# AdaLN/FFN with two adapter layers on one core: slot indices by one load, paced weight chunks, a bias folded to 64 partitions

## The chip, the cores and the metric

One Trainium2 chip, one NeuronCore of it. The metric is the device time of one execution in microseconds (us); lower is better. Engines: TensorE (PE, its weight loads PEld), VectorE (DVE), ScalarE (ACT), GpSimd (POOL) and SyncE (SP), which here does nothing but issue DMAs.

## The reference

The input x is (8 samples, 128 tokens, 512). Two layers follow each other without a nonlinearity, and the result is added to x:

```python
# layer 1: base product plus the adapter that each sample picks from 32 slots
y = x @ W.T + b  +  2.0 * (x @ lora_As[adapter_mapping]) @ lora_Bs[adapter_mapping]
# layer 2: base product plus 8 expert adapters of rank 16, weighted by a top-2 router
base   = y @ W_base.T + b_base
rw,sel = top_k(y @ W_router.T, 2);  w = softmax(rw) scattered over the 8 experts
lora   = sum_e w[e] * (y @ A[e].T) @ B[e].T * 2.0
out    = x + base + lora
```

## The kernel before

**What is tiled.** Nothing lies between the layers, so the kernel multiplies the weights together first. C is the second layer's right side: 280 columns of W_base.T, 8 router columns, 128 expert columns, 232 more of W_base.T, 648 in all (WC). `wt` holds W and C in four chunks of 128 rows, k = 0 to 3, each row also with the first layer's bias b repeated (CB = 1164 columns, 582 KB a chunk). Every operand is split into a rounded "high" part (fp32r) and a "low" remainder, and each product is three matmuls: high by high, high by low, low by high.

**The order on TensorE** is written out by hand, in stages:
1. 28 idle matmuls, then M = W.T C, per chunk k 24 matmuls (line 567). Chunk 0 comes in four pieces, of which SP and ACT issue two each. The last chunk goes block by block (i = 0 to 3), so that ACT can copy block i out of PSUM as high part (`bm`, `am`, line 330) and VectorE form its low part (line 408).
2. G = B-adapters by C, 24 matmuls (line 628, "the G product"). It waits for the adapters' high and low parts and for `m_lo_done` 2, the low parts of block 0 of M, since it writes in PSUM where that block stood.
3. The bias product (line 639): ones by `bsum_hl`, two column ranges, high and low: 4 matmuls. `bsum` is the sum over k of C row by b of that row (line 413, on VectorE, 4 steps), a matmul with ones adds up its 128 partitions. The second layer's bias b_base is put into `bsum`'s row 0 by a DMA ahead of the first step, on a tile that GpSimd has set to zero.
4. Per sample: `routed` (line 661, 12 matmuls of 384 columns) with router, expert and adapter columns; `plain` (line 673); the slot product (lines 696 and 701), which adds G's rows of the sample and the bias rows, both from the stack `g_st`; the transposes and the expert product (line 721). VectorE adds x (line 520), SP writes out.

**SP's queue** is one list in program order: pieces of w0, then w1, b_base, w2, w3, x0 (the transposed x of samples 0 and 1, 512 KB), then for each sample a load of its slot index into a register (line 233) and the DMA of its adapter (line 234, 64 KB), then x1, b_t, x2, x3 (lines 236 to 239). Later: 12 DMAs that build `g_st`, two that write bias rows to it (line 258), x by rows, and the outputs. Each DMA has a semaphore that the reader waits for.

**ACT's queue** around the change: high parts of chunks 1 to 3, of x0, of the adapters, of `bsum`, then of the blocks of M, of x1, of b_t, of G, of the bias product. **VectorE's**: low parts of the chunks with a bias step between, `bs_lo`, then the low parts of M, with `bsum`'s after block 1. **GpSimd**: waits for `bs_lo_done` and forms the adapters' low part (line 308), puts adapters beside M (line 304) and forms the low parts of x (line 297); `routed(0)` waits for the first two of these.

Of the kernel before, what the change touches and what calls it, by code (L numbers as in the profile page):

```python
# [32 lines left out]
P = 128  # L33
# [11 lines left out]
AHEAD = 4  # L45
CH = D + WC
# [10 lines left out]
GK = CROW + 2  # L57
# [11 lines left out]
def build(nc, x, xn_in, w, tbl, idx, bbase, bt, out):  # L69
    with ExitStack() as ctx:  # L70
# [29 lines left out]
        bsum_hl = sb("bsum_hl", [P, 2, WC], F32R)  # L100
# [10 lines left out]
        hw = sb("hw", [P, PAIRS, 2, P])  # L111
        hw_hi = sb("hw_hi", [P, NB, P], F32R)
# [49 lines left out]
        bsum_zero = sem("bsum_zero")  # L162
# [22 lines left out]
        m_lo_done = sem("m_lo_done")  # L185
        bsum_done = sem("bsum_done")
        bsum_hi_done = sem("bsum_hi_done")
# [3 lines left out]
        g_lo_done = sem("g_lo_done")  # L191
        c_done = sem("c_done")
# [27 lines left out]
        def _(sp):  # L220
# [15 lines left out]
            sp.dma_start(xt[:, 1], x[:, 1]).then_inc(x_in[1], 16)  # L236
            sp.dma_start(btt[:], bt).then_inc(bt_in, 16)
            for p in range(2, PAIRS):
                sp.dma_start(xt[:, p], x[:, p]).then_inc(x_in[p], 16)

            for p in range(PAIRS):
                rows = slice(2 * R * p, 2 * R * (p + 1))
                if p == 0:
                    sp.wait_ge(g_hi_done, 2)
                sp.dma_start(g_st[0:LROW, p, :].bitcast(F32),
                             g_hl[rows, 0, :].bitcast(F32)).then_inc(gst_in[p], 16)
                sp.dma_start(g_st[HROW:CROW, p, :].bitcast(F32),
                             g_hl[rows, 0, :].bitcast(F32)).then_inc(gst_in[p], 16)
                if p == 0:
                    sp.wait_ge(g_lo_done, 2)  # L250
                sp.dma_start(g_st[LROW:HROW, p, :].bitcast(F32),
                             g_hl[rows, 1, :].bitcast(F32)).then_inc(gst_in[p], 16)
                if p == 0:

                    sp.wait_ge(c_hi_done, 2)
                    sp.wait_ge(c_lo_done, 2)
                    for i in range(2):
                        sp.dma_start(g_st[CROW + i:CROW + i + 1, :, :].bitcast(F32),
                                     bsum_hl[0:1, i:i + 1, :].bitcast(F32).to_broadcast([1, PAIRS, WC])
                                     ).then_inc(cst_in, 16)  # L260
# [16 lines left out]
        def _(pool):  # L277
            nc.gpsimd.memset(bsum[:], 0.0).then_inc(bsum_zero, 1)
# [27 lines left out]
            pool.wait_ge(bs_lo_done, 1)  # L306
# [21 lines left out]
        def _(act):  # L328
# [11 lines left out]
            hi(wt_hi[:, 0, D + QB:CH], wt[:, 0, D + QB:CH]).then_inc(wc_hi_done, 1)  # L340

# [14 lines left out]
            x_high(0)  # L356
# [17 lines left out]
            for s, c in enumerate(COLS):  # L374
                hi(bsum_hl[0:1, 0, c], ps[0:1, C_BANK + s, 0:c.stop - c.start]).then_inc(c_hi_done, 1)
# [22 lines left out]
        def _(dve):  # L398
# [11 lines left out]
            def bias_sum(k):  # L410
                if k > 0:
                    dve.wait_ge(bsum_done, k)
# [15 lines left out]
            for k in range(1, KB):  # L428
# [10 lines left out]
                if k == 1:  # L439
                    dve.wait_ge(bbase_in, 16)  # L440
                bias_sum(k - 1)
            bias_sum(KB - 1)
            dve.wait_ge(ab_hi_done, 1)
            lo(bs_lo[:].rearrange("p k b r -> p b k r"), ab[:, :, 1],
               bs_hi[:].rearrange("p k b r -> p b k r")).then_inc(bs_lo_done, 1)

            for i in range(KB):
                if i == 2:
                    dve.wait_ge(bsum_hi_done, 1)
                    lo(bsum_hl[:, 1], bsum[:], bsum_hl[:, 0]).then_inc(bsum_lo_done, 1)  # L450
# [3 lines left out]
                lo(am[:, i, 1, R:R + WA], ps[:, 2 * i + 1, 0:WA], am[:, i, 0, R:R + WA]).then_inc(m_lo_done, 1)  # L454
            for s, c in enumerate(COLS):
                dve.wait_ge(g_hi_done, s + 1)
                lo(g_hl[:, 1, c], ps[:, G_BANK + s, 0:c.stop - c.start], g_hl[:, 0, c]).then_inc(g_lo_done, 1)
            for s, c in enumerate(COLS):
                dve.wait_ge(c_hi_done, s + 1)
                lo(bsum_hl[0:1, 1, c], ps[0:1, C_BANK + s, 0:c.stop - c.start],  # L460
                   bsum_hl[0:1, 0, c]).then_inc(c_lo_done, 1)
# [96 lines left out]
        def _(pe):  # L558
# [258 lines left out]
```

## Time and profile before

| what | value |
|---|---|
| times of three runs | 66.97, 67.73, 67.77 us, median 67.73 |
| the profiled execution | 67.57 us |
| its span, first to last instruction | 65.8 us |
| outside the span | 1.8 us |
| busy: PE, VectorE, ACT, GpSimd | 61.9, 35.9, 21.5, 17.0 us |
| granted TensorE clock over the span | 1.00, also in the 40 slices |

The span is the part that the rows explain; the time is the span and 1.8 us around it. A matmul's row shows its own duration, but matmuls overlap, so what one costs the stream is the distance from start to start. Positions below are microseconds from the start of the span.

### The profile page before, as it was taken

To read this page: it belongs to the slowest core of one execution; us is meant where nothing else is said; L and a number is where in the kernel's file an instruction comes from. 1 tells how busy PE (TensorE), PEld (TensorE's weight loads), DVE (VectorE), ACT (ScalarE), POOL (GpSimd) and SP (SyncE) were. 2 spreads that over 40 slices of the span, in tenths; PEclk is the share of its full clock that TensorE was granted. 3 is DMA by queue.
4 is the path that set the end of the run, shared out by engine and by line. 5 is a ranking of instruction groups with operands and counts; after the bars stand their busy time and mean duration, and the time that the engine had idled before them with its cause. 6 is when DMAs were issued, how large, how long until landed. Compare 5 with 4: busy or idle time off the path is not lost.

```text
span 65.8 us, 1181 instructions
## 1 busy us (share of the span) xinstructions
PE 61.9 (94%) x424; PEld 60.8 (92%) x424; DVE 35.9 (55%) x103; ACT 21.5 (33%) x46; POOL 17.0 (26%) x30
## 2 busy tenths in 40 slices
PE   5999979999999999999999999999999999999930
PEld 5979879999999999998999999999999999999920
DVE  0056289998599667015935495002668363857320
ACT  0660358905989399127104100010201040020000
POOL 6810000000699982695390000010100000000000
PEclk9999999999999999999999999999999999999999
DMA  0899998219999004245559999700044000013532
GB/s 0 247 376 259 393 411 262 71 54 175 217 356 369 25 0 101 60 104 129 123 136 339 275 283 401 267 15 0 0 159 159 10 0 0 0 66 123 215 146 87
DMA packets 5865, 10.55 MB, mean 160 GB/s; under 512 B 731, under 2 KB 2523, under 8 KB 5860
## 3 DMA queue, kind: packets, MB, share of 16 engines
q1 hardware_dynamic: 5570, 10.15, 48.0%
q10 hardware_dynamic: 290, 0.33, 1.5%
q8 instruction: 3, 0.05, 0.3%
q14 instruction: 2, 0.02, 0.1%
HBM read 7.37 MB, written 2.10 MB: 144 GB/s over the span
## 4 chain that ended last, share of the span: by engine, by line
PE 83%; DMA 9%; SPq 1%; ACT 1%; DVE 1%; issue 1%
PE ps L661 26%; PE ps L673 19%; PE ps L567 17%; DMA wt<-w_chunks 9%; PE ps L721 9%; PE ps L628 5%; PE ps L696 2%; PE ps L701 2%; PE ps L684 1%; PE ps L707 1%; SPq L223 1%; ACT wt_hi L330 1%; PE ps L639 1%; DVE xn L520 1%
## 5 line engine op out<-in xcount | busy, mean ns | idle before, releaser
L661 PE MATMUL ps<-am,x_hi 128*128 128x384 f32 x64 | 16.6, 340 | 0.0
L673 PE MATMUL ps<-bm,x_hi 128*128 128x280 f32 x64 | 13.0, 297 | 0.0
L661 PEld LDWEIGHTS ps<-am,x_hi 128*128 128x128 f32 x64 | 11.4, 188 | 0.0
L661 PE MATMUL ps<-am,x_lo 128*128 128x384 f32 x32 | 10.8, 338 | 0.0
L297 POOL TENSOR_TENSOR x_lo<-xt,x_hi 128x512 fp32r<-128x512 f32 x8 | 10.8, 1367 | 0.0
L673 PEld LDWEIGHTS ps<-bm,x_hi 128*128 128x128 f32 x64 | 10.2, 188 | 0.0
L673 PE MATMUL ps<-bm,x_lo 128*128 128x280 f32 x32 | 9.3, 291 | 0.0
L567 PE MATMUL ps<-wt_hi 128*128 128x280 f32 (+1 forms) x32 | 7.4, 327 | 0.5 <-ACT wt_hi L330 0.3
L520 DVE TENSOR_TENSOR xn<-ps,xn 128x280 f32<-128x280 f32 (+1 forms) x16 | 6.1, 418 | 2.4 <-PE ps L721 2.3
L567 PE MATMUL ps<-wt_lo,wt_hi 128*128 128x280 f32 (+1 forms) x32 | 7.0, 316 | 0.0
L567 PE MATMUL ps<-wt_hi,wt_lo 128*128 128x280 f32 (+1 forms) x32 | 6.5, 310 | 0.0
L408 DVE TENSOR_TENSOR wt_lo<-wt,wt_hi 128x512 fp32r<-128x512 f32 (+3 forms) x9 | 5.9, 689 | 0.8 <-ACT wt_hi L330 0.8
L304 POOL CAST am<-as_hl 128x128 fp32r<-128x128 f32 x8 | 2.3, 293 | 15.4 <-PE ps L661 15.4
L567 PEld LDWEIGHTS ps<-wt_hi 128*128 128x128 f32 x32 | 5.4, 196 | 1.0 <-DVE wt_hi L431 0.6
L673 PEld LDWEIGHTS ps<-bm,x_lo 128*128 128x128 f32 x32 | 6.0, 188 | 0.0
L330 ACT ACTIVATE hw_hi<-ps 128x256 fp32r<-128x256 f32 x4 | 1.5, 384 | 13.7 <-PE ps L707 13.7
L661 PEld LDWEIGHTS ps<-am,x_lo 128*128 128x128 f32 x32 | 6.0, 188 | 0.0
L330 ACT ACTIVATE wt_hi<-wt 128x648 fp32r<-128x648 f32 (+3 forms) x8 | 4.3, 573 | 4.1 <-DMA wt<-w_chunks 4.1
L567 PEld LDWEIGHTS ps<-wt_lo,wt_hi 128*128 128x128 f32 x32 | 5.4, 195 | 0.0
L408 DVE TENSOR_TENSOR hw_lo<-ps,hw_hi 128x256 fp32r<-128x256 f32 x4 | 1.7, 425 | 6.7 <-ACT hw_hi L330 6.7
L567 PEld LDWEIGHTS ps<-wt_hi,wt_lo 128*128 128x128 f32 x32 | 5.1, 188 | 0.0
L308 POOL TENSOR_TENSOR as_hl<-ab,as_hl 128x512 fp32r<-128x512 f32 x1 | 1.3, 1302 | 13.3 <-DVE bs_lo L408 13.3
(70 smaller groups left out, 98.5 us busy)
## 6 DMA issues: line engine op xcount, KB each, us to landing
xt<-x_t SPq DMA_DIRECT2D x4, 512.0 KB, 6.5
xn<-x_n SPq DMA_DIRECT2D x4, 512.0 KB, 6.0
out_n<-xn SPq DMA_DIRECT2D x7, 256.0 KB, 2.0
wt<-w_chunks SPq DMA_DIRECT2D x3, 582.0 KB, 6.6
g_st<-g_hl SPq DMA_DIRECT2D x12, 81.0 KB, 2.1
ab<-adapters SPq DMA_DIRECT2D x8, 64.0 KB, 2.7
wt<-w_chunks SPq DMA_DIRECT2D x2, 128.0 KB, 2.9
btt<-b_t SPq DMA_DIRECT2D x1, 256.0 KB, 5.0
```

What stands on the lines that cost most here:

```text
L297: nc.gpsimd.tensor_tensor(x_lo[:, p, k, :], xt[:, p, k, :], x_hi[:, p, k, :].bitcast(F32), ALU.subtract).then_inc(x_lo_done, 1)
L304: nc.gpsimd.tensor_copy(am[:, :, :, at:at + R], as_hl[:, b].bitcast(F32)).then_inc(as_put, 1)
L330: return nc.scalar.activation(dst, src, ACT.Copy)
L408: return nc.vector.tensor_tensor(dst, src, high.bitcast(F32), ALU.subtract)
L520: nc.vector.tensor_tensor(xn[:, b, c], src, xn[:, b, c], ALU.add).then_inc(out_ready, 1)
L567: return mm(ps[:, 2 * i + s, 0:cols.stop - cols.start], a[:, k, i * P:(i + 1) * P], c[:, k, D + cols.start:D + cols.stop], start=first, st ...
L628: last = mm(ps[:, G_BANK + s, 0:c.stop - c.start], a[:, k].rearrange("p b r -> p (b r)"), v[:, k, D + c.start:D + c.stop], start=(k == 0 a ...
L661: last = mm(a_bank(b)[:, 0:R + WA], v[:, p, i, tok], am[:, i, level, at:at + R + WA], start=(i == 0 and n == 0), stop=False, skip_group_ch ...
L673: mm(b_bank(b)[:, 0:QB], v[:, p, i, tok], bm[:, i, level, :], start=(i == 0 and n == 0), stop=False, skip_group_check=True)
L696: last = mm(a_bank(2 * p + t)[:, at:at + WA], h_t[0:GK, p, t, :], g_st[0:GK, p, QB:WC], start=False, stop=False, skip_group_check=True)
L701: mm(b_bank(b)[:, 0:QB], h_t[0:GK, b // 2, b % 2, :], g_st[0:GK, b // 2, 0:QB], start=False, stop=False, skip_group_check=True)
L721: last = mm(dst, v[:, b, :], m[:, c], start=False, stop=(n == 2), skip_group_check=True)
```

## The change

It does five things.
1. SP reads all eight slot indices by one load and then issues the eight adapter DMAs one behind the other.
2. SP issues w1, waits for the first piece of w0 (`w0_in[0]`), issues w2, waits for the indices and reads them, issues w3, then the adapters, and only then x0, x1, b_t, x2, x3 and b_base. ACT takes the adapters ahead of x0 to match.
3. The first bias step (k = 0) is an ACT activation with a scale per partition, so `bsum` need not be zero at the start; GpSimd's memset of it goes. VectorE keeps steps 1 to 3.
4. VectorE folds `bsum` to 64 partitions: it copies the upper half down (64x648), adds it, and the high part goes to partitions 0 to 63 and the low part to 64 to 127 of one tile `bsum_st`. The bias product is then 2 matmuls, not 4. High and low are made ahead of those of M, and GpSimd now starts after `bsum_lo_done`.
5. b_base goes to a row of its own. Its high part (ACT) and low part (VectorE) are formed after those of M and sent as two more rows of `g_st`, so the slot product has 100 rows, not 98, and waits for four such DMAs.

```diff
@@ SP @@
-            for k in range(1, KB):
-                sp.dma_start(wt[:, k, :], w[:, k, :]).then_inc(w_in[k], 16)
-                if k == 1:
-                    sp.wait_ge(bsum_zero, 1)
-                    sp.dma_start(bsum[0:1, :], bbase).then_inc(bbase_in, 16)
-            sp.dma_start(xt[:, 0], x[:, 0]).then_inc(x_in[0], 16)
-
+            sp.dma_start(wt[:, 1, :], w[:, 1, :]).then_inc(w_in[1], 16)
+            sp.wait_ge(w0_in[0], 16)
+            sp.dma_start(wt[:, 2, :], w[:, 2, :]).then_inc(w_in[2], 16)
             sp.wait_ge(idx_in, 16)
-            for b in range(NB):
-                slot = sp.value_load(idx_sb[0:1, b:b + 1], min_val=0, max_val=SLOTS - 1)
+            _, slots = nc.values_load_multi_w_load_instructions(
+                idx_sb[0:1, :], engines=[mybir.EngineType.SP], min_val=0, max_val=SLOTS - 1)
+            sp.dma_start(wt[:, 3, :], w[:, 3, :]).then_inc(w_in[3], 16)
+            for b, slot in enumerate(slots):
                 sp.dma_start(ab[:, b].rearrange("p c k r -> p (c k r)"),
                              tbl[bass.ds(slot, 1)].rearrange("s p n -> (s p) n")).then_inc(ab_in, 16)
+            sp.dma_start(xt[:, 0], x[:, 0]).then_inc(x_in[0], 16)
             sp.dma_start(xt[:, 1], x[:, 1]).then_inc(x_in[1], 16)
             sp.dma_start(btt[:], bt).then_inc(bt_in, 16)
             for p in range(2, PAIRS):
                 sp.dma_start(xt[:, p], x[:, p]).then_inc(x_in[p], 16)
+            sp.dma_start(bb, bbase).then_inc(bbase_in, 16)
+            sp.wait_ge(bb_hi_done, 1)
+            spread(CROW, bb_hl[:, 0:1, :])
+            sp.wait_ge(bb_lo_done, 1)
+            spread(CROW + 1, bb_hl[:, 1:2, :])
@@ ACT @@
+            act.wait_ge(w0_in[2], 16)
+            nc.scalar.activation(bsum[:], wt[:, 0, D:CH], ACT.Copy,
+                                 scale=wt[:, 0, CH:CH + 1]).then_inc(bsum_first, 1)
...
-            x_high(0)
             act.wait_ge(ab_in, 16 * NB)
             hi(bs_hi[:].rearrange("p k b r -> p b k r"), ab[:, :, 1]).then_inc(ab_hi_done, 1)
             hi(as_hl[:, :, :, 0, :], ab[:, :, 0]).then_inc(ab_hi_done, 1)
-            act.wait_ge(bsum_done, KB)
-            hi(bsum_hl[:, 0], bsum[:]).then_inc(bsum_hi_done, 1)
+            x_high(0)
+            act.wait_ge(halves_done, 1)
+            hi(bsum_st[0:HP], bsum[0:HP]).then_inc(bsum_hi_done, 1)
...
+            act.wait_ge(bbase_in, 16)
+            hi(bb_hl[:, 0], bb).then_inc(bb_hi_done, 1)
             x_high(1)
@@ VectorE @@
-                bias_sum(k - 1)
+                if k > 1:
+                    bias_sum(k - 1)
             bias_sum(KB - 1)
+            dve.wait_ge(bsum_done, KB - 1)
+            nc.vector.tensor_copy(upper, bsum[HP:P]).then_inc(upper_done, 1)
+            dve.wait_ge(upper_done, 1)
+            nc.vector.tensor_tensor(bsum[0:HP], bsum[0:HP], upper, ALU.add).then_inc(halves_done, 1)
             dve.wait_ge(ab_hi_done, 1)
             lo(bs_lo[:].rearrange("p k b r -> p b k r"), ab[:, :, 1],
                bs_hi[:].rearrange("p k b r -> p b k r")).then_inc(bs_lo_done, 1)
+            dve.wait_ge(bsum_hi_done, 1)
+            lo(bsum_st[HP:P], bsum[0:HP], bsum_st[0:HP]).then_inc(bsum_lo_done, 1)
 
             for i in range(KB):
-                if i == 2:
-                    dve.wait_ge(bsum_hi_done, 1)
-                    lo(bsum_hl[:, 1], bsum[:], bsum_hl[:, 0]).then_inc(bsum_lo_done, 1)
...
+            dve.wait_ge(bb_hi_done, 1)
+            lo(bb_hl[:, 1], bb, bb_hl[:, 0]).then_inc(bb_lo_done, 1)
@@ GpSimd @@
-            nc.gpsimd.memset(bsum[:], 0.0).then_inc(bsum_zero, 1)
...
-            pool.wait_ge(bs_lo_done, 1)
+            pool.wait_ge(bsum_lo_done, 1)
@@ TensorE @@
-                for i in range(2):
-                    last = mm(ps[:, C_BANK + s, 0:c.stop - c.start], ones_r[:], bsum_hl[:, i, c],
-                              start=(i == 0), stop=(i == 1))
+                last = mm(ps[:, C_BANK + s, 0:c.stop - c.start], ones_r[:], bsum_st[:, c], start=True, stop=True)
...
-                    pe.wait_ge(cst_in, 32)
+                    pe.wait_ge(cst_in, 64)
```

SP's queue at the head of the program, before: `w_chunks` are w1 and, behind b_base, w2 and w3; ISA rows are register operations on a slot index.

```order
L225 DMA wt<-w_chunks 128x1164
L228 DMA bsum<-b_base 1x648 [waits bsum_zero]
L225 DMA wt<-w_chunks 128x1164 x2
L229 DMA xt<-x_t 128x1024
L233 TENSOR_LOAD idx_sb [waits idx_in]
L233 ISA x2
L234 ISA
L234 DMA ab<-adapters 128x128
L233 TENSOR_LOAD idx_sb
```

And the same place in the changed kernel:

```order
L233 DMA wt<-w_chunks 128x1164
L235 DMA wt<-w_chunks 128x1164 [waits w0_in0]
L237 TENSOR_LOAD idx_sb [waits idx_in]
L237 ISA x16
L239 DMA wt<-w_chunks 128x1164
L241 ISA
L241 DMA ab<-adapters 128x128
```

b_base and x0 have left this place. The eight loads have become one with sixteen register operations, and these stand ahead of w3's issue and of all adapters; x0's issue follows the eighth adapter.

ACT's queue from chunk 3 to the first block of M, before (`bs_hi` and `as_hl` are the adapters, `bm` and `am` block 0 of M):

```order
L330 ACTIVATE wt_hi<-wt 128x648 [waits w_in3]
L330 ACTIVATE wt_hi<-wt 128x512
L330 ACTIVATE x_hi<-xt 128x512 [waits x_in0]
L330 ACTIVATE x_hi<-xt 128x512
L330 ACTIVATE bs_hi<-ab 128x8x4x16 [waits ab_in]
L330 ACTIVATE as_hl<-ab 128x32x16
L330 ACTIVATE bsum_hl<-bsum 128x648 [waits bsum_done]
L330 ACTIVATE bm<-ps 128x280 [waits m_done]
```

And in the changed kernel:

```order
L345 ACTIVATE wt_hi<-wt 128x648 [waits w_in3]
L345 ACTIVATE wt_hi<-wt 128x512
L345 ACTIVATE bs_hi<-ab 128x8x4x16 [waits ab_in]
L345 ACTIVATE as_hl<-ab 128x32x16
L345 ACTIVATE x_hi<-xt 128x512 [waits x_in0]
L345 ACTIVATE x_hi<-xt 128x512
L345 ACTIVATE bsum_st<-bsum 64x648 [waits halves_done]
L345 ACTIVATE bm<-ps 128x280 [waits m_done]
```

The wait for x0 has moved behind the one for the adapters; it is now the last DMA wait in the queue ahead of the bias and of block 0 of M.

## Rows read from the trace of the kernel before

**Rows 1.** The chain in order of time: start us, length us, what.

```profile
1.66 6.05 DMA wt<-w_chunks
...
8.62 10.92 PE ps L567 x72
19.54 3.56 PE ps L628 x24
23.10 0.60 PE ps L639 x4
```

**Rows 2.** Timeline of PE and PEld at chunk 1 and G: start, length, what, idle before.

```profile
6.95 1.34 PE L567 MATMUL ps<-wt_hi,wt_lo 128*128 128x280 f32 x8
8.62 0.75 PE L567 MATMUL ps<-wt_hi 128*128 128x280 f32 x4 [0.33 <-ACT wt_hi L330]
...
19.21 0.19 PEld L628 LDWEIGHTS ps<-wt_hi,bs_hi 128*128 128x128 f32 x1
```

**Rows 3.** DMA queues, window 0 to 5.5 us: packets, MB, share of 16 engines.

```profile
q1 hardware_dynamic: 430, 0.86, 53.0%
```

**Rows 4.** Timeline of SP's queue: x0, the adapters, x1.

```profile
3.39 1.13 SPq L229 DMA_DIRECT2D xt<-x_t  x1
5.56 8.44 SPq L234 DMA_DIRECT2D ab<-adapters  x8
14.04 0.43 SPq L236 DMA_DIRECT2D xt<-x_t  x1
```

**Rows 5.** Source lines 233 and 234: ns min/median/max, first and last start.

```profile
L233 SPq TENSOR_LOAD <-idx_sb x8: 262/269/487, 4.6 to 12.6; - x8
L233 SPq FUSED_REGOPS  x8: 152/152/192, 5.1 to 12.9; - x8
...
L234 SPq FUSED_REGOPS  x8: 42/42/48, 5.4 to 13.1; - x8
...
L234 SPq DMA_DIRECT2D ab<-adapters x8: 337/338/714, 5.6 to 13.3; - x8
```

**Rows 6.** Issue to landing, line 225: w1, w2, w3.

```profile
DMA to landing us min/median/max: 6.0/6.6/7.7
```

**Rows 7.** Issue to landing, line 236: x1.

```profile
DMA to landing us min/median/max: 4.9/4.9/4.9
```

**Rows 8.** Issue to landing, line 262, window 32.9 to 33.5: the first of x by rows.

```profile
DMA to landing us min/median/max: 3.8/3.8/3.8
```

**Rows 9.** Issue to landing, line 239: x2 and x3, issued at 15.0 and 15.5.

```profile
DMA to landing us min/median/max: 6.2/6.5/6.9
```

**Rows 10.** Timeline of ACT: start, length, what, idle before it.

```profile
9.19 1.27 ACT L330 ACTIVATE wt_hi<-wt 128x648 fp32r<-128x648 f32 x2 [0.71 <-DMA wt<-w_chunks]
10.64 1.27 ACT L330 ACTIVATE wt_hi<-wt 128x648 fp32r<-128x648 f32 x2 [0.18 <-DMA wt<-w_chunks]
11.96 1.16 ACT L330 ACTIVATE x_hi<-xt 128x512 fp32r<-128x512 f32 x2
...
16.56 0.73 ACT L330 ACTIVATE bsum_hl<-bsum 128x648 fp32r<-128x648 f32 x1
...
23.14 0.77 ACT L330 ACTIVATE g_hl<-ps 128x280 fp32r<-128x280 f32 x2 [1.22 <-PE ps L628]
```

**Rows 11.** Timeline of VectorE: the last chunk's bias steps, block 0 of M.

```profile
14.16 1.81 DVE L413 SCALAR_TENSOR_TENSOR bsum<-wt,bsum 128x648 f32<-128x648 f32 x2
...
17.61 0.45 DVE L408 TENSOR_TENSOR bm<-ps,bm 128x280 fp32r<-128x280 f32 x1 [0.75 <-ACT bm L330]
17.98 0.54 DVE L408 TENSOR_TENSOR am<-ps,am 128x368 fp32r<-128x368 f32 x1
```

**Rows 12.** Groups by form: busy us, mean ns of one, idle before.

```profile
L408 DVE TENSOR_TENSOR wt_lo<-wt,wt_hi 128x648 fp32r<-128x648 f32 x3 | 2.5, 827 | 0.3 <-ACT wt_hi L330 0.3
L431 DVE CAST wt_hi<-wt 128x512 fp32r<-128x512 f32 x1 | 0.4, 427 | 1.5 <-DMA wt<-w_chunks 1.5
```

**Rows 13.** Timeline of GpSimd: the adapters' low part.

```profile
16.95 1.30 POOL L308 TENSOR_TENSOR as_hl<-ab,as_hl 128x512 fp32r<-128x512 f32 x1 [13.34 <-DVE bs_lo L408]
```

More of the change, by code:

```diff
@@ L45 @@
 AHEAD = 4
+HP = P // 2
 CH = D + WC
@@ L56 @@
 LROW, HROW, CROW = 2 * R, 4 * R, 6 * R
-GK = CROW + 2
+GK = CROW + 4
 AW = R + WA + R
@@ L99, in build @@
         bsum = sb("bsum", [P, WC])
-        bsum_hl = sb("bsum_hl", [P, 2, WC], F32R)
+        bsum_st = sb("bsum_st", [P, WC], F32R)
+        cb_hl = sb("cb_hl", [HP + 1, 2, WC], F32R)
+        c_hl, bb_hl = cb_hl[0:1], cb_hl[HP:HP + 1]
         h_stack = sb("h_stack", [P, PAIRS, 2 * HSTEP])
@@ L111, in build @@
         hw = sb("hw", [P, PAIRS, 2, P])
+        hw_flat = hw[:].rearrange("p a t c -> p (a t c)")
+        upper, bb = hw_flat[0:HP, 0:WC], hw_flat[HP:HP + 1, 0:WC]
         hw_hi = sb("hw_hi", [P, NB, P], F32R)
@@ L160, in build @@
         bbase_in = sem("bbase_in")
-        bsum_zero = sem("bsum_zero")
         const = sem("const")
@@ L185, in build @@
         m_lo_done = sem("m_lo_done")
+        bsum_first = sem("bsum_first")
         bsum_done = sem("bsum_done")
+        upper_done = sem("upper_done")
+        halves_done = sem("halves_done")
         bsum_hi_done = sem("bsum_hi_done")
@@ L191, in build @@
         g_lo_done = sem("g_lo_done")
+        bb_hi_done = sem("bb_hi_done")
+        bb_lo_done = sem("bb_lo_done")
         c_done = sem("c_done")
@@ L239, in _, with spread @@
                 sp.dma_start(xt[:, p], x[:, p]).then_inc(x_in[p], 16)
+            sp.dma_start(bb, bbase).then_inc(bbase_in, 16)
+            def spread(row, src):
+                sp.dma_start(g_st[row:row + 1, :, :].bitcast(F32),
+                             src.bitcast(F32).to_broadcast([1, PAIRS, WC])).then_inc(cst_in, 16)
+            sp.wait_ge(bb_hi_done, 1)
+            spread(CROW, bb_hl[:, 0:1, :])
+            sp.wait_ge(bb_lo_done, 1)
+            spread(CROW + 1, bb_hl[:, 1:2, :])
             for p in range(PAIRS):
@@ L257, in _ @@
                     for i in range(2):
-                        sp.dma_start(g_st[CROW + i:CROW + i + 1, :, :].bitcast(F32),
-                                     bsum_hl[0:1, i:i + 1, :].bitcast(F32).to_broadcast([1, PAIRS, WC])
-                                     ).then_inc(cst_in, 16)
+                        spread(CROW + 2 + i, c_hl[:, i:i + 1, :])
             for p in range(PAIRS):
@@ L374, in _ @@
             for s, c in enumerate(COLS):
-                hi(bsum_hl[0:1, 0, c], ps[0:1, C_BANK + s, 0:c.stop - c.start]).then_inc(c_hi_done, 1)
+                hi(c_hl[0:1, 0, c], ps[0:1, C_BANK + s, 0:c.stop - c.start]).then_inc(c_hi_done, 1)
             x_high(2)
@@ L410, in bias_sum @@
             def bias_sum(k):
-                if k > 0:
-                    dve.wait_ge(bsum_done, k)
+                if k == 1:
+                    dve.wait_ge(bsum_first, 1)
+                else:
+                    dve.wait_ge(bsum_done, k - 1)
                 nc.vector.scalar_tensor_tensor(out=bsum[:], in0=wt[:, k, D:CH], scalar=wt[:, k, CH:CH + 1],
@@ L438, in _ @@
                 lo(wt_lo[:, k, 0:D], wt[:, k, 0:D], wt_hi[:, k, 0:D]).then_inc(w_lo_done, 1)
-                if k == 1:
-                    dve.wait_ge(bbase_in, 16)
-                bias_sum(k - 1)
+                if k > 1:
+                    bias_sum(k - 1)
             bias_sum(KB - 1)
+            dve.wait_ge(bsum_done, KB - 1)
+            nc.vector.tensor_copy(upper, bsum[HP:P]).then_inc(upper_done, 1)
+            dve.wait_ge(upper_done, 1)
+            nc.vector.tensor_tensor(bsum[0:HP], bsum[0:HP], upper, ALU.add).then_inc(halves_done, 1)
             dve.wait_ge(ab_hi_done, 1)
@@ L459, in _ @@
                 dve.wait_ge(c_hi_done, s + 1)
-                lo(bsum_hl[0:1, 1, c], ps[0:1, C_BANK + s, 0:c.stop - c.start],
-                   bsum_hl[0:1, 0, c]).then_inc(c_lo_done, 1)
+                lo(c_hl[0:1, 1, c], ps[0:1, C_BANK + s, 0:c.stop - c.start],
+                   c_hl[0:1, 0, c]).then_inc(c_lo_done, 1)
             dve.wait_ge(bt_hi_done, 1)
```

## The prediction

> **What bounds the kernel now.** Read the chain of waits first, in order of time [rows 1]. It opens with a DMA, chunk w1, from its issue at 1.66 to its landing 6.05 later, at 7.71. From 8.62 on the chain is matmuls with hardly a break: M to 19.54, the G product to 23.10, the bias product to 23.70, then the samples. So the time is where TensorE starts chunk 1, plus the length of its stream, plus any wait inside it. Everything else counts only if it becomes such a wait.
>
> Then read TensorE's timeline at chunk 1 [rows 2]. The 8 last matmuls of chunk 0 start at 6.95. A full third of a chunk (8 matmuls) takes 10.92 / 9 = 1.21 us of stream [rows 1], so they leave the stream free at about 8.15, and chunk 1 starts at 8.62. The gap is 0.47 us, and w1's landing with ACT's high part behind it ends it. That is all that an earlier w1 can give.
>
> **The change, part by part.** The sum is made against the profiled 67.57 us.
>
> *Bias product, 4 matmuls to 2.* The four took 0.60 us of stream [rows 1]; one of each width goes, so half: **-0.30 us**, on the chain. This one is sure.
>
> *Pacing, for w1.* To start chunk 1 at 8.15, w1 must be in by about 7.2, since from its landing to the first matmul of chunk 1 it was 0.91 us (7.71 to 8.62). Between **0 and -0.47 us**. For a gain: 0.86 MB had passed SP's queue by 5.5 us [rows 3], which is its two pieces of w0 (0.26 MB) and w1 (0.60 MB), yet w1 landed at 7.71. Some of its transfers were held up while w2, w3 and x0 lay behind it; with w2 issued 1 us later and the others much later, the hold-up may go. Against it: w2 is issued before w1 is through in either kernel. I can't choose by these rows; what each end makes of the sum shows below, where a later wait takes a part of it back.
>
> On this point the Trainium skill, DMA: Bandwidth & Descriptors, section Queues, rings and completion order, says that each DMA engine consumes a ring's descriptors in ring order. By that rule what is queued behind w1 can't slow it and pacing gives 0; the trace agrees in the bytes of [rows 3], not in the landing 2.2 us after them. By the rule the sum would be 67.3; if the landing row is right and the hold-up goes, 67.1.
>
> *Index load and the queue on SP.* This is where I look for the cost. Before, the adapters' issues were 7.7 / 7 = 1.10 us apart [rows 5], of which the load is 0.27, the register operation on it 0.15, the one on the address 0.04 and the issue 0.34; the remaining 0.30 is an assert, a move and the gaps. Now: w2's issue ends at about 4.0; the first load started at 4.6, when x0's issue had ended, so the indices are in by then, and I take 4.6. The load takes 0.49 as the first did: 5.1. Then eight pairs of register operations. Upper bound 0.15 + 0.12 a value, 2.2 us in all; lower bound, if the 0.15 was mostly a wait for the load, 0.04 + 0.12, 1.3 us. I take 1.8: w3 is issued at 6.9 instead of about 3, and takes 0.47. Eight adapters at 0.04 + 0.34 + 0.15 = 0.53 are 4.2: x0 is issued at **11.5**, not at 3.39 [rows 4]. The ends are 11.1 and 12.0.
>
> *When x0 lands, and who waits.* The nearest row is x1 before: 512 KB too, issued at 14.04 right behind the adapters' trickle, landed 4.9 us later [rows 4, 7]. The next is the first x by rows, into an idle queue: 3.8 [rows 8]. As a lower bound: ACT took w2 and w3 at 9.19 and 10.64 [rows 10], 1.45 a chunk when queued back to back, so 512 KB move in 1.3; an adapter of 64 KB was in by about 2.2 (the last issued at 13.3, waited for until 15.5), which makes 3.3. I take 3.9, between the two rows nearer the quicker one, because the queue is never quite empty now: x0 lands at **15.4** (14.4 to 16.9).
>
> Behind x0 in ACT's queue stand its own high part, the bias, and block 0 of M, and behind these, in VectorE's, bias low, `bm` low, `am` low; the G product waits for the last of them. From the landing: x0's two operations 1.08 (1.16 less the overlap) [rows 10], the bias high part 0.73, its low part 0.83 [rows 12], `bm` to `am` 0.37 and `am` 0.54 [rows 11], and about 0.08 of hand-over: **3.63 us**. So G can start at 15.4 + 3.63 = 19.0. TensorE's first weight load of G stood at 19.21 [rows 2], right behind the last of M, and comes at 18.74 if w1 gives its 0.47. Thus G is held to about 19.0 with an early w1, and not held with a late one (19.21). The gain at G is 0.2 or 0: with the bias product, **-0.5 or -0.3**; I take -0.4.
>
> *Bias chain.* VectorE loses one step of 0.9 (half of 1.81 [rows 11]); ACT takes it at 0.75 while it waits for w1 anyway. Added are a copy of 64x648 (0.50: 427 ns for 512 columns [rows 12], scaled), an addition and a low part at 0.83 each, against a low part of 648 columns that stood between blocks 1 and 2 of M. The chain after w3: ACT 0.76, VectorE 1.43 of low parts, bias steps 1.8, copy and addition 1.3: 5.3. With w3 landing at 10.6 as before, and VectorE busy with chunk 2 until then, the halves are done between 16.2 and 16.9; x0's high part is through at 16.5. The two arrive together, so neither hides more than some 0.4 us of the other's lateness. GpSimd starts when `bsum_lo` is done, at about 18.1, not 16.95 [rows 13]. Its 5 us until the first two low parts of x were ready by 21.9 and needed at 23.5; now 23.1 against a need at about 22.9 to 23.1 (G at 19.0 to 19.2, its 3.56 and the bias product's 0.30 [rows 1]). Taken as 0, bound +0.3.
>
> *b_base.* It is last in SP's line, behind x3, which landed at 15.5 + 6.9 = 22.4 [rows 9]; x1 to x3 now follow x0 from 12 on, so x3 and b_base come at about 21.5. ACT reaches the wait at about 20.3 and stands; then b_base high 0.7, x1 1.1, b_t 0.6, so G's high part starts at 23.9 instead of 23.14 [rows 10], where 1.22 us were idle. The bias rows reach `g_st` that much later; they had over 1 us in hand before the first slot product (landing about 28.7, product at 30.15). I take 0, bound +0.8. SP's two more DMAs of 0.65 fall where it waits for G. Two more rows in the slot product add no columns: 0.
>
> Sum: 67.57 - 0.30 - 0.1 = **67.2 us**. The profiled execution lies 0.16 below the median of the runs, so a median may come out at 67.3 as well. What a measurement of this kernel can tell from no change is about 2%, here 1.35 us.
>
> **Rivals.**
>
> *A, everything in time.* w1 lands by 7.2 and x0 by 15.1, as it would at 11.5 + 3.3 = 14.8. Then -0.47 and -0.30: 66.8. For it the bytes of [rows 3]; against it x1's 4.9 us. The Trainium skill, DMA: Bandwidth & Descriptors, section Anatomy of one DMA, gives 2.0 us plus bytes over 436 GB/s (a fit for GpSimd's path); an estimate by that page is 3.2 us for 512 KB, x0 in at 14.7. The trace does not agree for x1 (4.9) or the first x by rows (3.8).
>
> *B, no earlier w1, x0 in time.* The change does not do what its pacing says: 67.3, all from the bias product. It lies so close to the forecast that only the trace tells them apart: chunk 1 still starts near 8.6.
>
> *C, slower: x0 gates G.* x0's landing repeats x1's 4.9 us: in at 16.4, or 16.9 with the late issue. G starts at 20.0 to 20.5, 0.8 to 1.3 after 19.21; less 0.30: 68.1 to 68.6, say 68.2. It costs more than the change brings from a landing at about 15.9 on. For it: the nearest row of all, with the same trickle ahead. Against it: x0 itself moved at full rate when it followed the chunks. A w3 that takes its 6.6 us [rows 6] from 6.9 on would land at 13.5 and do the same through the bias chain, its limit being about 11.6; then 69 or more.
>
> *D, b_base holds the first slot product.* b_base in after 22.4: at 23.2, 0.8 us of wait: 68.0.
>
> **How the numbers follow.** The forecast, x0 near 15.4 so that G starts at 19.0 to 19.2, 0.25; B 0.25 (its time, 67.3, falls in the forecast's own 67.0 to 67.4, so that 67.2 is the likeliest time with 0.5); A 0.17; C 0.25, of which 0.07 by w3 and dearer than 2%; D 0.08. Eight in ten lie between 66.4 and 68.8: A with a little more at the low end, C with the late issue at the high end. Faster by over 2% (below 66.4) would need more than A: 0.06. Slower by over 2% (above 69.1): 0.10. Within: 0.84.
>
> **What would show it.** Right: the bias product's row x2 and 0.30; SP's x0 issue between 11.1 and 12.0 and its landing in 3.3 to 4.9; one block of register operations of 1.3 to 2.2 between load and w3. If G's first matmul starts later than chunk 3's last by more than 0.17, x0 or the halves gate it, and ACT's idle time ahead of `x_hi` or `bsum_st` tells which. Wrong: a TensorE wait anywhere else (first slot product: D; `routed(0)`: GpSimd), or an x0 issued before 10, which would mean that I have misread the register operations. The prediction fails if w3 lands after 11.6, or if the stream's start moves by more than the 0.47 us that the gap holds.

## The result and the profile after

| | before | after |
|---|---|---|
| first comparison, 4 runs each | median 67.64 us (66.97 to 67.77) | 68.87 us (68.12 to 70.84) |
| ratio, 95% interval | | 1.018 (1.010 to 1.026) |
| the same two kernels again (a0) | 67.36 us, 13 runs | 69.12 us, 5 runs; 1.026 (1.017 to 1.035) |
| the profiled execution: time, span, outside it | 67.57, 65.8, 1.8 us | 70.84, 68.7, 2.1 us |

The changed kernel is slower, by about 2%. The forecast of 67.2 us was wrong. The mechanism that came true is rival C, with two costs on top that no case held. In the profiled execution the granted clock fell for 3.4 us. That cost 1.6 us and explains 70.84 (last section); the other three had a clock of 1.0 over the span and took 68.12, 68.66 and 69.08. The medians here and below hold all executions; the ratios compare fast ones with fast ones, so without those in which the clock fell.

The chain of the changed kernel in order of time (start, length, what), to be held against [rows 1]:

```profile
11.76 5.57 DMA xt<-x_t
17.35 1.15 ACT x_hi L345 x2
21.07 5.34 PE ps L653 x24
26.71 5.26 PE ps L684 x30
```

In [rows 1] only matmuls stand from 8.62 to 23.70. Here the chain leaves TensorE, goes through x0's DMA from its issue at 11.76 to its landing at 17.33, and comes back at the G product, 21.07. SP's queue shows how x0 came to be issued there [rows 4 for before]:

```profile
3.42 0.33 SPq L235 DMA_DIRECT2D wt<-w_chunks  x1
7.23 0.33 SPq L239 DMA_DIRECT2D wt<-w_chunks  x1
7.75 3.96 SPq L241 DMA_DIRECT2D ab<-adapters  x8
11.76 0.43 SPq L243 DMA_DIRECT2D xt<-x_t  x1
```

Source line 237, the one load with its register operations (ns, first and last start in us), against [rows 5]:

```profile
L237 SPq FUSED_REGOPS  x8: 147/147/192, 5.1 to 7.0; - x8
L237 SPq SEQ_ASSERT  x8: 18/18/33, 5.4 to 7.2; - x8
L237 SPq TENSOR_LOAD <-idx_sb x1: 729/729/729, 4.4 to 4.4; - x1
```

Source line 243, x0, against [rows 7]:

```profile
DMA to landing us min/median/max: 5.6/5.6/5.6
```

Then ScalarE's timeline, where x0 is waited for, against [rows 10]:

```profile
15.56 0.62 ACT L345 ACTIVATE as_hl<-ab 128x512 fp32r<-128x512 f32 x1
17.35 1.15 ACT L345 ACTIVATE x_hi<-xt 128x512 fp32r<-128x512 f32 x2 [1.17 <-DMA xt<-x_t]
18.41 0.73 ACT L345 ACTIVATE bsum_st<-bsum 64x648 fp32r<-64x648 f32 x1
19.04 0.38 ACT L345 ACTIVATE bm<-ps 128x280 fp32r<-128x280 f32 x1
```

VectorE's, against [rows 11]:

```profile
16.45 0.68 DVE L427 TENSOR_TENSOR bs_lo<-ab,bs_hi 128x512 fp32r<-128x512 f32 x1
19.17 0.83 DVE L427 TENSOR_TENSOR bsum_st<-bsum,bsum_st 64x648 fp32r<-64x648 f32 x1 [2.04 <-ACT bsum_st L345]
20.03 0.45 DVE L427 TENSOR_TENSOR bm<-ps,bm 128x280 fp32r<-128x280 f32 x1
20.39 0.53 DVE L427 TENSOR_TENSOR am<-ps,am 128x368 fp32r<-128x368 f32 x1
```

And TensorE's at the end of M, at G and at the bias product, against [rows 2]:

```profile
18.80 0.33 PE L592 MATMUL ps<-wt_hi,wt_lo 128*128 128x368 f32 x1
21.07 0.37 PE L653 MATMUL ps<-wt_hi,bs_hi 128*128 128x280 f32 x1 [1.94 <-DVE am L427]
...
26.25 0.46 PE L663 MATMUL ps<-bsum_st,ones_r 128*128 128x280 f32 x2
26.55 0.52 PE L684 MATMUL ps<-am,x_hi 128*128 128x384 f32 x2
```

These rows form one staircase. ScalarE stands 1.17 us for x0 while block 0 of M lies ready in PSUM behind it from about 16.4 on (chunk 3 starts at 15.40, and a quarter of it takes 0.9). VectorE stands 2.04 us for ScalarE, and TensorE 1.94 us for VectorE. The bias product is x2 and 0.30 us from start to start, as forecast.

The whole difference in the span, 2.91 us, from positions in the two traces (before, after): chunk 1 starts at 8.62, 8.20: -0.42. M keeps its length. From M's last matmul to G: 0.17, 2.27: +2.10. G: 3.56, 5.18: +1.62 (the clock). Bias product to `routed(0)`: 0.59, 0.30: -0.29. The rest, 42.26 and 42.16: -0.10. Outside the span it is 0.36 more.

### The profile page after: what moved, and what is told of

The parts are those of the page before. It is cut to its first block, busy times and chain, and to the rows that moved or that the text cites. A ratio compares the mean times of both kernels' runs of the same rounds, so it can differ in the third digit from the quotient of the medians.

```text
span 68.7 us, 1175 instructions
## 1 busy us (share of the span) xinstructions
PE 63.2 (92%) x422; PEld 61.9 (90%) x422; DVE 37.6 (55%) x105; ACT 22.8 (33%) x48; POOL 16.5 (24%) x29
## 4 chain that ended last, share of the span: by engine, by line
PE 65%; DMA 12%; SPq 8%; DVE 3%; issue 3%; ACT 3%; ACTq 1%
PE ps L684 25%; PE ps L696 18%; PE ps L744 8%; DMA xt<-x_t 8%; PE ps L653 8%; SPq L241 5%; DMA idx_sb<-slots 4%; SPq L237 3%; PE ps L719 2%; ACT x_hi L345 2%; PE ps L724 2%; PE ps L730 1%; PE ps L707 1%; ACTq L348 1%; DVE bsum_st L427 1%
```

## The experiments

All times are compared within one comparison. "Outside" is the time less the span: 1.73 to 1.83 us in every run of the kernel before.

### Which half of the change: a0, b1, e4, e3

a0 is the changed kernel again, b1 the kernel before; a0's 1.026 stands in the table above.

> The changed kernel unchanged, for its spread and for a second profile. Theory T1: x0, now issued at 11.8 us behind the index load, w3 and eight adapters, lands at about 17.3, and ACT's x0 high part, the bias, and block 0 of M wait behind it, so that the G product starts at landing + 3.7 us. T1 expects that relation again (G's first matmul 3.6 to 3.8 us after x0's landing), whatever the landing is; 1.0 to 1.5% slower than before. Theory T2: the longer bias chain on VectorE (two more steps, and low part ahead of those of M) gates G. T2 expects ACT to have x0's high part ready before the halves are done, and G at halves + 4 us. Second question: the granted clock fell after the 1.9 us wait in the first profile. If the wait alone does it, it falls again; if not in every execution, this profile may show 1.00 and a time near 68.6 us.

b1 had chunk 1 at 8.58, G at 19.36, a span of 65.8 and 67.55 us: the trace of before repeats.

> The kernel before, for a second profile. Its spans in the last comparison fell between 65.0 and 66.0 us, and the share of the time outside the span was 1.73 to 1.82 us in all 13 runs. Theory: the spread comes from the start, where the granted clock rises at another moment and w1 lands at another, so chunk 1 should start between 8.1 and 8.7 us here too, and everything after it take the same time as in the first profile (57.2 us from chunk 1 to the end), within 0.1 us. Rival: the spread comes from waits later in the stream.

e4 is the queue half on the kernel before (load, order of SP, ScalarE's x0 behind the adapters; bias as before):

> Before's bias (4 matmuls, no folding, b_base in row 0 of bsum, 4 steps on VectorE) with the changed DMA order, single index load and ACT order. Theory T1 (the queue costs, the bias part is neutral): x0 issued at about 12.1 (one DMA more ahead), landing at about 17.3, G at landing + 1.1 (x0 high) + 0.7 (bias high) + 1.3 (block 0 high and low) = 20.4, 1.2 us late; time 68.6 to 69.0 us, and the granted clock may fall after the wait. Theory T4: the part of the time outside the span, 2.13 us in every run with the changed bias against 1.77, belongs to the bias part; then it is 1.77 here. If it belongs to the queue part it is 2.13 here (against which e3 speaks already).

**68.35 us, ratio 1.012 (1.006 to 1.017)**, outside 1.73 to 1.81. Its TensorE timeline:

```profile
18.56 0.33 PE L568 MATMUL ps<-wt_hi,wt_lo 128*128 128x368 f32 x1
20.56 0.37 PE L629 MATMUL ps<-wt_hi,bs_hi 128*128 128x280 f32 x1 [1.67 <-DVE am L409]
```

x0 landed at 17.37. So the queue half alone makes the wait.

e3 is the bias half alone, with SP's old queue:

> Before's DMA order and index loads (all chunks and x0 first, one load per slot, x0's high part ahead of the adapters' on ACT) with the changed bias: first step on ACT, folding, two matmuls, b_base as rows, its DMA at the end of the line. T1: the bias part alone is worth its 0.30 us less what the longer chain takes: adapters landed 15.5, ACT free for the bias at 16.6, bias low at 18.1, G at 19.2 to 19.4; time 67.2 to 67.7 us against before's 67.6. T2: G starts after 20, and this kernel carries most of the loss: 68.4 us or more.

67.34 us, 1.002 (0.996 to 1.007). From chunk 1 to the end of the span it took 57.01 us, before 57.17, but outside it 2.09 to 2.21 us.

### Where x0 stands: e1, e5, e2

```diff
@@ e1: SP @@
             sp.dma_start(wt[:, 3, :], w[:, 3, :]).then_inc(w_in[3], 16)
+            sp.dma_start(xt[:, 0], x[:, 0]).then_inc(x_in[0], 16)
             for b, slot in enumerate(slots):
...
-            sp.dma_start(xt[:, 0], x[:, 0]).then_inc(x_in[0], 16)
@@ e5: the same, and on ACT x_high(0) ahead of the adapters @@
@@ e2: SP as changed; on ACT x_high(0) behind the blocks of M @@
```

> The changed kernel with x0's DMA issued right after w3's, ahead of the eight adapters; nothing else moves. T1: x0 is issued at about 7.6 us and lands by 12.5, out of the way; the adapters go 0.47 us later and land by about 15 us, so the bias high part starts when the halves are done (about 16.5), G starts by 19.4 to 19.6, and the time is 66.8 to 67.4 us, 1 to 2 us under the changed kernel. T2: G stays late, at 20.5 or more, and the time above 68 us.

e1: 68.72 us, 1.021 (1.008 to 1.034): I had expected 66.8 to 67.4. x0 landed at 13.06, but ScalarE's queue still had x0 behind the adapters, which landed at 15.39, so both were worked off after 15.39:

```profile
20.19 0.37 PE L653 MATMUL ps<-wt_hi,bs_hi 128*128 128x280 f32 x1 [0.59 <-DVE am L427]
```

The wait at G fell from 1.94 to 0.59 us and did not go: x0 landed 4.3 us earlier, and G gained 1.35. An earlier landing brings only a part where the reader's queue keeps its order.

> The changed kernel with x0 issued ahead of the adapters and with ACT's x0 high part ahead of the adapters' too. In e1 x0 landed at 13.1 but its high part still stood behind the adapters (landed 15.4), so G had to wait for adapters + 1.1 + 1.1 + bias. T1: now only 1.1 (adapters' high parts) stands there, the halves are done at about 17.0, G starts 0.1 to 0.5 us behind the last of M; time 67.3 to 67.8 us, about 1 us under the changed kernel. T2 (the bias chain itself is too long): G still 0.6 us or more behind, 68.2 or more.

e5: with both queues turned, x0 landed at 12.72, and G followed M's last matmul by 0.28 us, not 2.27. 68.02 us, 1.011 (1.004 to 1.017). The ratio stands for about 0.7 us, of which 0.36 is outside the span (2.09 to 2.21) again. The rest, about 0.3 us, I can't assign: from chunk 1 to the end of the span the profiled execution, the fastest of the four, took 56.92 us against 57.17 in before.

> The changed kernel with ACT's high part of x0 moved behind the high parts of M's four blocks; x0 lands as late as in the changed kernel. T1: what cost the time is the position in ACT's queue, not the landing itself, so G starts at about 19.3 (halves done 16.5, bias high and low 1.6, block 0's low parts 1.0, hand-over), and the time is 66.9 to 67.6 us; ACT's x0 part ends at about 21 and GpSimd's low parts of x0 at about 23, just ahead of the first sample's product. T2: no better than the changed kernel. A third theory, T3: the late x0 would then hold routed(0) itself, so that the wait only moves from G to there and the time stays at 68.5.

e2: x0 landed late again, at 17.00, but G was on time (19.21, 0.17 behind M). TensorE's list of waits, 17 to 35 us:

```profile
PE ps L684 <- POOL x_lo L312: 1.0, 1, 1.0
```

The wait has moved to `routed(0)`, which needs the low part of x0. 68.37 us, 1.015 (1.006 to 1.025). e5 and e2 together show that G's wait was x0's high part in ScalarE's queue. The new wait is again one of place in that queue: x0 was in at 17.00, and ScalarE, busy with the four blocks of M, took it up at 20.07. A place between, behind block 0 of M alone, was not tried, so it stays open what a late x0 costs at its best place.

### The parts of the bias half: f1, f2, f3, s1

f1 has the fold alone (b_base in `bsum`'s row 0, four bias steps on VectorE), f2 b_base's rows alone (bias product x4), f3 is f2 with the first step on ScalarE and without GpSimd's memset. s1 adds to before four semaphores and four tiny GpSimd memsets that raise them, and nothing else.

> Before's DMA queue, all four bias steps on VectorE and b_base in bsum's row 0 as before; only the folding to 64 partitions and the bias product of 2 matmuls are new. The changed bias showed 2.09 to 2.21 us outside the span where before shows 1.73 to 1.83, and four more semaphores alone did not (s1: 1.73 to 1.83). Theory T5a: the folding (copy to other partitions, half-height operations) brings it: 2.1 outside. T5b: the rows of b_base or ACT's first step bring it: 1.77 here. On the stream: -0.30 us from the bias product; with one bias step more on VectorE than the changed kernel, the halves are done at 17.2 and G is held 0.3 to 0.6 us; sum about zero, 67.2 to 67.9 us.

f1: 67.37, 1.001 (0.997 to 1.004), outside 1.73 to 1.82. The fold gives its 0.30 and takes it back: its low part is ahead of M's in VectorE's queue, and TensorE waits 0.53 us at G.

> Before's DMA queue and bias product (4 matmuls, no folding, four steps on VectorE from a zeroed bsum), with b_base as two more rows of the slot product, its DMA last in the line. T5b: if these rows bring the 0.36 us outside the span, 2.1 outside and 67.8 to 67.9 us; if not, 1.77 and 67.5. The stream itself should not change, unless ACT's wait for b_base (landing about 21) reaches the first slot product, which I expect it not to.

f2: 68.02, 1.011 (1.002 to 1.021), outside **1.98 to 2.08**.

> f2 with the first bias step on ACT (activation with a scale per partition), no memset of bsum. Theory T5c: this instruction brings the 0.36 us outside the span (2.1 here, 1.77 in f2). If f2 already shows 2.1, then no more here. Time otherwise as f2, VectorE 0.9 us less busy before the G product, which nothing waits for.

f3: 68.12, 1.014 (1.005 to 1.022), outside **2.09 to 2.21**.

> The kernel before with four more semaphores, each raised once by a one-column memset at the end of GpSimd's queue, where it is idle. The changed kernel has four more than before. Theory T4a: the 0.36 us more outside the span are a cost per semaphore (about 0.09 us each), so this kernel shows 2.1 us outside and takes 0.3 to 0.4 us more than before. Rival T4b: they come from something else of the bias part (another kind of instruction, tile sizes); then 1.77 outside, and no difference in time.

s1: 67.24, 0.996 (0.992 to 0.999), outside 1.73 to 1.83. Not the number of semaphores.

### Pacing alone: p1

```diff
                 if k == 1:
...
+                    sp.wait_ge(w0_in[0], 16)
```

> The kernel before with one edit: SP waits for the first piece of w0 before it issues w2 (so w2, w3 and x0 are issued 1 to 1.5 us later). Theory P1 (pacing lets w1 in earlier): w1 lands by 7.1 to 7.4, as in the six paced profiles (7.06 to 7.38), instead of 7.66 to 7.71, chunk 1 starts 0.1 to 0.45 us earlier depending on when the granted clock rises, and the time is 0.2 to 0.3 us under before. Rival P2 (w1's landing varies by itself: two kernels without pacing showed 7.16 and 7.32): no difference of the medians, within 0.1 us.

67.33, 0.999 (0.995 to 1.003). w1 landed at 7.46. In thirteen profiles without pacing it landed anywhere from 7.07 to 8.13, in the seven paced ones between 7.06 and 7.46. Seven of the thirteen lie above 7.46, none of the seven, so w1 does come somewhat earlier when paced. But the time can't be told from no change; the interval leaves room for 0.3 us. One reason is in the other profiles. In six of the thirteen (e3, f2, g2, s1, q1, q2) chunk 1 starts 1.18 to 1.20 us after the last third of chunk 0, so TensorE did not wait for w1 at all, and there was no gap to close.

### What lies outside the span: q1, q2, q3, e6

q1 writes two bias rows more to `g_st` by DMA, in rows that nobody reads. q2 and q3 add to before one dummy activation of 128x512 ahead of w1's high part, with and without a scale per partition; SP waits for it before it issues b_t, whose tile it writes. All three only add work.

> The kernel before with two more bias DMAs on SP, high and low row of bsum copied once more into two rows of g_st that nobody reads, and a wait for them at the end of SP's queue. Dummy work is added and nothing else changes. If the part outside the span grows with the number of DMAs (or semaphores waited for by SP), it is 1.95 to 2.1 us here against 1.73 to 1.83 before; if the b_base rows brought their 0.25 us otherwise, it stays at 1.73 to 1.83. Span unchanged within 0.3 us, ratio 1.003 to 1.006 or 1.000.

q1: 67.13, 0.997 (0.994 to 1.000), outside 1.74 to 1.84: not the DMAs.

```diff
@@ q2: ACT @@
+            act.wait_ge(w0_in[2], 16)
+            nc.scalar.activation(btt[:], wt[:, 0, D:2 * D], ACT.Copy,
+                                 scale=wt[:, 0, CH:CH + 1]).then_inc(scaled, 1)
@@ q3: the same without the scale @@
```

> The kernel before with one more activation on ScalarE: 128x512 of w0 times a scale per partition (the first layer's bias column), written to the b_t tile before b_t's own data are loaded. Dummy work is added and nothing else changes. If an activation with a scale per partition makes the part outside the span longer (it was 0.1 more in the run of rows and ACT step than in rows alone), it is 1.85 us or more here; if that was something else, it stays at 1.73 to 1.83. The activation itself should take about 0.6 us in ScalarE's wait for w1, so the span stays within 0.3 us, ratio 0.998 to 1.006.

q2: 67.62, 1.005 (1.001 to 1.009), outside **1.99 to 2.08**.

> As the run of the scaled activation, with a plain copy of the same 128x512 in its place (no scale per partition). Dummy work is added and nothing else changes. Theory N (the part outside the span goes by the number of ScalarE's activations in the program: 46 gave 1.73 to 1.83 us in seven kernels, 47 gave 1.98 to 2.08, 48 gave 2.09 to 2.21, whatever the activation did): 47 activations, 1.98 to 2.08 us outside. Rival S (the scale per partition brings it): 1.73 to 1.83.

q3: 67.47, 1.002 (0.998 to 1.006), outside **2.02 to 2.08**: the scale is not the cause either. By then the number of activations fitted every kernel, so e6 takes two away from e3 by joining the high parts of x2 and of x3:

```diff
-                for k in range(0, KB, 2):
-                    hi(x_hi[:, p, k:k + 2, :], xt[:, p, k:k + 2, :]).then_inc(x_hi_done, 1)
+                step = KB if p > 1 else 2
+                for k in range(0, KB, step):
+                    hi(x_hi[:, p, k:k + step, :], xt[:, p, k:k + step, :]).then_inc(x_hi_done, step // 2)
```

> The whole bias part of the change with the kernel's old queue (as in e3, 48 activations on ScalarE), but the high parts of x2 and of x3 are one activation of 1024 columns each, not two of 512, so that ScalarE has 46 again. Theory N: outside the span falls from 2.09 to 2.21 to 1.73 to 1.83 us, the span stays that of e3 (chunk 1 to the end about 57.0), median about 67.0, ratio 0.993 to 0.998. Rival (b_base's rows and the first bias step bring it by what they do): it stays at 2.09 to 2.21, ratio 1.000 to 1.003.

e6: 68.05, 1.011 (1.005 to 1.017), outside still 2.09 to 2.17 with 46 activations. So the number of activations does not fit. Two other counts still fit every kernel. One is ScalarE's waits for DMAs: 11 in the kernels with 1.72 to 1.84, 12 in f2, q2 and q3 (1.98 to 2.08), 13 in e3, f3, e6 and the changed kernel with e1, e2 and e5 (2.09 to 2.22). The other is all of ScalarE's instructions in the trace, semaphore waits that stand as instructions of their own included: 53, 54 and 55 in the same groups. e6 did not lower it, since the trace has two such waits ahead of the joined activations (at 23.92 and 24.01) where the two activations went. No run parts the two counts or takes a wait away by itself, so both stay correlations.

### The fold alone, its parts made later: g1, g2

g1 is f1 with the folded bias's high and low parts behind block 1 of M, and GpSimd waits for `bs_lo` again; g2 is g1 with e6's joined activations.

```diff
@@ g1 against f1: ACT @@
-            act.wait_ge(halves_done, 1)
-            hi(bsum_st[0:HP], bsum[0:HP]).then_inc(bsum_hi_done, 1)
             for i in range(KB):
+                if i == 2:
+                    act.wait_ge(halves_done, 1)
+                    hi(bsum_st[0:HP], bsum[0:HP]).then_inc(bsum_hi_done, 1)
```

> The kernel before with the fold alone (b_base in bsum row 0, all bias steps on VectorE, the bias product 2 matmuls), its high and low part made behind block 1 of M and GpSimd released by bs_lo, as before. Theory T (only the PE stream and the waits in it count, the 0.48 us wait of the first fold run was the folded bias standing ahead of M's low parts): the G product starts within 0.2 us of the last matmul of M, bias product 0.30 us, span 0.30 shorter than before at an equal start of chunk 1 (chunk 1 to the end about 56.9, not 57.17), outside the span 1.72 to 1.83, median 67.0 to 67.2, ratio 0.993 to 0.998. Rival R (the bias part arrives later and is waited for between G and the bias product or at the first slot product): G on time but bias product or slot product late by 0.3 or more, ratio 1.00 or above.

> g1 (the fold alone, made behind block 1 of M) with the high parts of x2 and of x3 as one activation each, so ScalarE has 44 activations instead of 46. Theory N with a term per activation: outside the span below 1.73 us, perhaps 1.5 to 1.7, median 66.8 to 67.0, ratio 0.990 to 0.996. Theory N with a step between 46 and 47 only: 1.73 to 1.83, same as g1, ratio 0.996 to 0.999. This is the candidate for a version that beats both kernels.

g1: 67.18 us against 67.26, 0.997 (0.994 to 1.000). g2: 67.17 against 67.43, 0.997 (0.993 to 1.000). In both the G product follows M's last matmul by 0.17 us, and outside is as before, 1.73 to 1.84. g2's chain from chunk 1 on:

```profile
19.79 3.56 PE ps L642 x24
23.34 0.30 PE ps L652 x2
```

Both lie 2 to 3% under the changed kernel, compared through the kernel before. Against the kernel before each interval just reaches 1.000, and s1 and q1, which only add work to it, came out at 0.996 and 0.997 too. So the times show no gain. The traces do: from chunk 1 to the end of the span g1 took 56.99 us and g2 56.69, against 57.17 and 57.19 in the two profiles of before and 57.10 in s1 and q1, but that is one execution each. Two activations fewer changed nothing outside the span; ScalarE's instructions are 53 in g2 as in g1.

## Why the prediction was wrong

**What came as written.** The bias product: 0.30 off, from x4 to x2. SP's queue: the load from 4.38, the block of register operations 2.1 us long (1.3 to 2.2 given, 1.8 taken: the upper bound was right, each of the eight takes 0.15 as a chained one did), w3 issued at 7.23 (6.9), x0 at 11.76 (11.5; 11.1 to 12.0). That the load ended at 5.11, as written, is luck: it took 0.73 us, not 0.49, and began 0.22 earlier than I took. From x0's landing to G 3.74 us (3.63). w3 landed at 11.17, ahead of the 11.6 that was its limit, and the halves were done before x0's high part was. b_base held nothing (D did not occur): G to the first slot product is otherwise unchanged. In the profiled execution chunk 1 started at 8.20, close to the 8.15 of rival A.

**The step that failed: "I take 3.9 ... x0 lands at 15.4."** It is the term for x0's landing; from it the sum had G at 19.0 to 19.2, with no wait. x0 landed 5.6 us after its issue, at 17.33. In e4, a0 and e2, with the same order on SP, it took 5.5, 5.3 and 5.4. I had the nearest row in hand, x1 with 4.9 us behind the same trickle [rows 7], and moved away from it toward a DMA into an idle queue [rows 8] with the reason that the queue is "never quite empty now". That row was itself the low end: in the fourteen profiles with SP's old order x1 took 4.66 to 5.75 us, and the 5.3 to 5.6 of x0 lie inside that. The trace shows what the reason missed. Windows of the changed kernel (us, busy time of each engine, PEclk, DMA share, GB/s):

```profile
12.00:14.00 2.00, 2.00 (x15) 2.00 (x15) 2.00 (x3) 0.46 (x1) 0.00 (x0) 1.00 0.89 180
14.00:16.00 2.00, 2.00 (x16) 2.00 (x15) 1.90 (x4) 0.98 (x2) 0.00 (x0) 1.00 0.83 285
16.00:17.40 1.40, 1.40 (x11) 1.40 (x10) 1.12 (x2) 0.23 (x2) 0.00 (x0) 1.00 0.98 357
```

From 12.0 to 17.4 the DMA engines moved 1.43 MB (2.0 x 180, 2.0 x 285 and 1.4 x 357), and x0 has 0.52. Ahead of x0 stand 2.91 MB (w0 to w3 and the adapters), of which 2.78 had moved by 12.0, so 0.13 MB, two adapters' worth, still came first. The remaining 0.78 MB belong to x1, b_t and x2, issued behind x0 from 12.23 on: x0 was not waiting for its own bytes alone, and x1 was in only 1.24 us after it. And the first 2 us ran at half the rate of the last window though the DMA engines were 0.89 busy. In before, x1's second stretch after the trickle was slow as well, with all adapters in by 15.48. Window of before:

```profile
16.00:18.00 2.00, 2.00 (x16) 2.00 (x16) 1.08 (x3) 2.00 (x6) 1.05 (x1) 1.00 0.92 212
```

Such a slow start does not need small DMAs ahead. In the changed kernel w3, issued at 7.23 with weight chunks alone ahead of it, began in the same way while the queue had run nearly dry (0.14 busy from 7.0 to 8.0):

```profile
8.00:9.00 1.00, 0.97 (x7) 0.83 (x7) 0.91 (x2) 0.31 (x2) 0.00 (x0) 1.00 0.85 140
9.00:10.00 1.00, 1.00 (x9) 1.00 (x8) 1.00 (x2) 1.00 (x2) 0.00 (x0) 1.00 0.92 354
```

So w3, x0 and x1 of before each started below the rate that they reached later; why is not shown. In e1 and e5, where x0 was issued right behind w3, it took 5.4 and 5.3 us all the same, with w3's bytes ahead of it. With 4.9 taken, the sum was rival C's: 68.1 to 68.6. With the measured 5.6 its own arithmetic gives x0 in at 11.76 + 5.57, G at 17.33 + 3.63 = 20.96, 1.75 after 19.21, and 67.57 + 1.75 - 0.30 = 69.0. With the 0.36 of the next paragraph that is 69.4; the profiled 70.84 less the clock's 1.62 is 69.2. In the executions without a profile x0's landing is not known.

**A term that was not in the sum.** I wrote the sum "against the profiled 67.57 us" and changed only the span, as if the 1.8 us outside it were constant. It grew by 0.36 us with the bias half: by 0.25 with b_base's rows (f2) and 0.1 more with the first step on ScalarE (f3), which more than eats the 0.30 of the fold. This is why e3 is neutral. Without it the three executions at full clock (median 68.66) would be at 68.3, and the four of a0 (68.74 to 69.22, median 69.06) at 68.7, about C's 68.1 to 68.6.

**Pacing.** I could not choose between 0 and -0.47, and p1 finds no gain that can be measured. The Trainium skill, DMA: Bandwidth & Descriptors, section Queues, rings and completion order, says that a DMA engine takes a ring's descriptors in ring order; by that rule pacing would bring 0. p1's ratio of 0.999 agrees, while w1's landings, none of the paced later than 7.46, speak somewhat against it; no run decides. The start of chunk 1 that I read as one number, 8.62, varies by itself from 8.12 to 9.04 in the unpaced profiles, and moves the span with it. With x0 late such a gain is worthless anyway: G is set by x0's landing, and an earlier M only lengthens the wait.

**Rivals.** C came true with its place and who waits; its price fell short by the 0.36 us outside the span, and in the profiled execution by the later landing (5.6, not 4.9) and the clock too; it had a chance of 0.25, and the nearest row spoke for it. A's early w1 came in the profile and was lost in the wait, and B and D did not happen.

## What to carry to other kernels

Take a DMA's landing from the nearest row, the one with the same size behind the same kind of traffic, and move away from it only with a second row. Moving a load behind others is priced at its landing, and then along the reader's queue: look at what stands behind the waiting instruction there, since e1 (x0 early, read late) and e2 (x0 late, read late) each left a wait, and only e5 turned both. Read a landing from more than one profile: x1's 4.9 us was one draw from 4.7 to 5.8. Check on each run whether the time outside the span has moved: a gain of 0.3 us can be lost there, where no row of the trace shows it. And run the kernel with dummy work added as a control: a ratio of 0.997 is no gain when s1 has 0.996.

## What was not expected of the hardware

**The clock fell after the wait.** Windows of the changed kernel around G (same columns, PEclk third from the end):

```profile
21.00:22.00 1.00, 0.93 (x7) 0.96 (x8) 1.00 (x3) 0.98 (x4) 0.94 (x4) 0.93 0.02 8
22.00:25.30 3.30, 3.30 (x14) 3.30 (x14) 3.09 (x5) 2.18 (x4) 3.30 (x3) 0.50 0.01 3
25.30:27.00 1.70, 1.70 (x12) 1.70 (x11) 0.12 (x1) 0.56 (x2) 1.70 (x2) 1.00 0.02 6
```

TensorE stood idle from about 19.1 to 21.07, ran again at 1.00, and was then granted 0.50 (1.2 of 2.4 GHz) from 21.9 to 25.3, in the middle of busy matmuls; G took 5.18 us, not 3.56. It happened in 1 of 4 runs of the changed kernel, 1 of 5 of a0 (there from 21.0 to 24.4) and 1 of 4 of e1, which took 70.84, 70.63 and 70.90 us; in no run of any other kernel, whose clock over the span is 0.996 to 1.0, e4 with its wait of 1.67 us in the profile included. Two kernels tell against a simple rule: e4 had 1.67 us of wait and no fall in four executions, e1 had 0.59 us in its profile and a fall in another execution, whose own waits are not known. What is shown is that in the two profiled cases the fall followed waits of 1.94 and 1.84 us and cost 1.6 us more. That the wait is the cause was not tried by itself.

**Time outside the span** went in steps: 1.72 to 1.84, 1.98 to 2.08, 2.09 to 2.22 us. Not DMAs (q1), semaphores (s1), a scale (q3 against q2) or the number of activations (e6) made it; one dummy activation with its own wait for a DMA made the first step (q3). Whether it is the wait or the one instruction more on ScalarE stays open.
